# The mixing stage's normalised rows one place sooner in the loop that all engines share

## What is computed

```python
h = jnp.maximum(_layernorm(x, axis=-1), 0.0)
x = x + _L0_gnn_ref(h, adj, ...)      # attention, 16 heads
h = jnp.maximum(_layernorm(x, axis=-1), 0.0)
x = x + _L1_gnn_ref(h, adj, ...)      # two steps of spreading and of top-p attention
h = jnp.maximum(_layernorm(x, axis=-1), 0.0)
x = x + _L2_gnn_ref(h, adj, ...)      # attention, 8 heads, then four dense layers
h = jnp.maximum(_layernorm(x, axis=-1), 0.0)
x = x + _L3_gnn_ref(h, adj, ...)      # relations
```

```python
# end of L1: Z holds the sums of both steps
Y = X + Z
mu = Y.mean(axis=-1, keepdims=True)
var = Y.var(axis=-1, keepdims=True)
return (Y - mu) * jax.lax.rsqrt(var + LN_EPS) * gamma + beta
# next: x = x + that;  h = relu(_layernorm(x));  and of L2:
Wh = jnp.einsum('nf,hfd->hnd', x, W)
e_src = jnp.einsum('hnd,hd->hn', Wh, a1)
e_dst = jnp.einsum('hnd,hd->hn', Wh, a2)
```

## Time and profile before

| what | value |
|---|---|
| median of 3 runs | 3774.04 us |
| the three runs | 3775.52, 3774.04, 3762.97 us |
| the profiled execution | 3772.07 us, its span 3770.3 us |
| mean granted TensorE clock | 0.952 |
| busy share of the span | PE 90%, DVE 85%, ACT 75%, POOL 37% |
| the stage of the change | about 2328 to 2465 us of the span |

### The profile page before, as it was taken

The page is one execution under the profiler, slowest core; times in us unless marked ns, Lnnn a source line. Parts: engine busy times, 40 slices in busy tenths (PEclk is TensorE's granted clock), DMA queues, the critical chain, the costliest instruction groups (busy, mean ns, idle before and its releaser), DMA issues. The chain is left out here.

```text
span 3770.3 us, 56703 instructions
## 1 busy us (share of the span) xinstructions
PE 3378.9 (90%) x20628; PEld 2047.1 (54%) x20628; DVE 3201.0 (85%) x5502; ACT 2818.1 (75%) x3508; POOL 1389.7 (37%) x1048
## 2 busy tenths in 40 slices
PE   7799999986968976899999975989999898999999
PEld 3699999743434433444444432468888443444444
DVE  3699999679999999599999998389998414999996
ACT  5699999559999999389999982368776334666664
POOL 0387444104555556136565552145552110000000
PEclk9999999998989988999999987999999999999999
DMA  6721111120111113221101022410100211111110
GB/s 234 269 84 31 31 36 25 52 70 27 54 32 42 42 44 102 78 81 46 39 20 28 26 73 70 154 26 21 21 22 10 86 72 61 48 51 56 48 51 17
DMA packets 166328, 224.45 MB, mean 60 GB/s; under 512 B 90418, under 2 KB 102672, under 8 KB 162928
## 3 DMA queue, kind: packets, MB, share of 16 engines
q1 hardware_dynamic: 147152, 178.22, 15.1%
q0 software_dynamic: 18896, 42.46, 3.5%
HBM read 148.36 MB, written 72.00 MB: 58 GB/s over the span
## 5 line engine op out<-in xcount | busy, mean ns | idle before, releaser
L1819 DVE SCALAR_TENSOR_TENSOR adjT<-adjT,mid 128x2048 bf16<-128x2048 f32 x440 | 1034.8, 2352 | 13.9
L604 ACT ACTIVATE steepz<-s1b,thr_h 128x512 bf16<-128x512 f32 (+1 forms) x928 | 774.3, 915 | 32.5 <-DVE A L675 20.3
L1715 ACT ACTIVATE adjT<-adjT,nmid 128x2048 bf16<-128x2048 f32 x250 | 498.4, 1994 | 3.4 <-POOL nmid L1757 3.4
L1719 ACT ACTIVATE adjT<-adjT 128x2048 bf16<-128x2048 bf16 x250 | 477.9, 1912 | 6.0
L758 PE MATMUL acc<-V,B 128*128 128x198 bf16 x4096 | 442.5, 251 | 34.2 <-DVE B L677 14.1
L765 PE MATMUL acc<-V,adjT 128*128 128x99 bf16 (+1 forms) x5248 | 415.5, 217 | 0.0
L1773 POOL TENSOR_SCALAR reach<-above,lack 128x1 f32<-128x1 f32 x202 | 234.2, 1159 | 472.9 <-ACT lack L1722 472.7
L1775 POOL TENSOR_SCALAR nmid<-reach,steps,nmid 128x1 f32<-128x1 f32 x202 | 369.4, 1829 | 21.2
L765 PEld LDWEIGHTS acc<-V,adjT 128*128 128x128 bf16 x5248 | 340.5, 98 | 40.2 <-issue 0.7
L758 PEld LDWEIGHTS acc<-V,B 128*128 128x128 bf16 x4096 | 341.2, 98 | 37.6 <-issue 23.3
L1574 PE MATMUL psX<-parts,block 128*128 128x512 bf16 x1536 | 347.9, 382 | 10.5 <-POOL ident L209 4.1
(11 more groups left out here) (322 smaller groups left out, 6214.2 us busy)
## 6 DMA issues: line engine op xcount, KB each, us to landing
rows<-in_adj_dram SPq DMA_DIRECT2D x16, 1024.0 KB, 8.3
s1b<-sT_dram SPq DMA_DIRECT2D x32, 512.0 KB, 3.7
block<-adj_dram SPq DMA_DIRECT2D x32, 512.0 KB, 4.4
plain_table<-rows POOLq DMA_DIRECT2D x16, 512.0 KB, 8.1
adj_dram<-adjT POOLq DMA_DIRECT2D x4, 2048.0 KB, 21.6
veil_table<-fill POOLq DMA_DIRECT2D x64, 128.0 KB
y_dram<-yo SPq DMA_DIRECT2D x32, 256.0 KB, 2.0
adjT<-adj_dram SPq DMA_DIRECT2D x4, 2048.0 KB, 16.4
```

The lines of the kernel that those rows point to most:

```text
L604: act.activation(steepz[:, m % RELUS, :], s1b[:, q % 4, :], ACT.Relu, bias=thr_h[:, u, 1, j:j + 1], scale=STEEP).then_inc(relu_ready, 1)
L1715: act.activation(junk_s[:, u, :], expd[:, slot[i], :], ACT.Relu, bias=col(nmid, i), accum_out=col(above, i)).then_inc(sums_ready, 1)
L1719: act.activation(junk_s[:, u, :], junk_s[:, u, :], ACT.Sign, accum_out=col(over, i)).then_inc(sums_ready, 1)
L1819: link(dve.scalar_tensor_tensor(junk[:, :], e, col(mid, i), e, ALU.is_gt, ALU.mult, accum_out=found))
```

## The change

One number changes. `SOON` is 6 in place of 7 (LAG is 9), and with it `BEHIND` is 9 in place of 10 and the place of the last scores (`SOON + NT`) 22 in place of 23. The places of the late tiles' turns and sums, and all of VectorE's, GpSimd's and SyncE's order, stay.

```diff
             psS = psT[:, 0, :, :].rearrange("p k i -> p (k i)")[:, 0:NT * 2 * H].rearrange("p (t h) -> p t h", t=NT)
             m2 = psO[:, 1, 0:H]
-            SOON = LAG - 2
+            SOON = LAG - 3
             BEHIND = SOON + 3
             scored = {18 - 2: 0, 20 - 2: 1, 22 - 2: 2, SOON + NT: 3}
```

## The result

| | before | after |
|---|---|---|
| median, 9 executions each | 3772.60 us | 3787.28 us |
| lowest and highest | 3762.97, 3777.34 us | 3777.90, 3792.59 us |
| the profiled execution | 3772.07 us | 3792.59 us |
| the stage of the change | 137.81 us | 152.49 us |

The ratio is 1.0038, with a 95% interval of 1.0028 to 1.0047: slower, by 14.7 us. It grew by 14.68 us in the two profiled executions. That this is the difference of the medians to 0.01 us is chance: by the interval the medians differ by 10.6 to 17.7 us, and the length of a stage scatters too, as the experiments show.

What follows compares the result with a forecast made beforehand. TensorE's first start, work and idle time bound the stage. New stretches 6.35 + 6.78, less 4.44 gained, give +8.7 us; the clock's 4.4 makes +13.1, from 3774.04 to 3787.1, taken as 3787.0 us; range 3778 to 3792.

Steps and rivals of the forecast that it cites:

- The line of 0.3%: Whole kernel: a measurement can tell about 0.3%, 11.3 us, from no change; the forecast lies just beyond.
- The stage lasts as long as first start, work and idle time.: TensorE in the stage: the change alters no operation, so only first start (2352.50 us) and idle stretches can move time.
- The first start does not move.: Stage start: relu 0 still waits for VectorE's offsets, so the first turn keeps its time; put at zero.
- 4.44 us go.: Old TensorE idle stretches ahead of turns 3, 4 and 7 go or are counted anew: 1.74 + 0.54 + 2.16 us gained.
- 6.35 and 6.78 us come.: New TensorE idle stretches ahead of turn 4 (behind O9) and turn 8 (behind O12), waiting for group factors.
- The clock, 4.4 us.: Behind both new stretches TensorE's clock falls to half; matmuls there cost 2.2 us more each, +4.4 us.
- GpSimd meets VectorE in both chains.: GpSimd's addition again meets VectorE's `nmr` in both chains, keeping it at 1.20 us, not 0.16; 2.1 us in all.
- faster: Rival at relu 4: factors ready when O9 ends, old stretches go and none come; 3769.6 us, chance 0.03.
- The clock holds: Rival behind the new stretches: idle time comes as computed, clock stays full; +8.7 us, 3782.7 us, chance 0.11.
- More than two stretches: Rival in the stage: a shifted late sum opens a third idle stretch; +19.5 us, 3793.5 us, chance 0.06.
- The next stage absorbs it: Rival behind the stage: attention waits for the adjacency matrix, so a later end is free; 3774 us, chance 0.04.
- One sign that the prediction set: Outside the stage: the forecast is wrong if other stages differ by more than 2 us.

Runs made afterwards that it cites:

- The first experiment: Changed kernel, but VectorE takes the factors of tiles 4 to 7 ahead of its look at tile 9; stage 141.56 us, median 3776.86 us, ratio 0.9998.
- The kernel with both loops opened: Changed kernel, VectorE taking factors of tiles 4-7 before look 9, of 8-11 before look 12; GpSimd's additions for tiles 7, 11, 15 wait for factors; 3766.80 us.
- the filler: Changed kernel plus six unused 128x512 float32 products on TensorE ahead of turn 4 and of turn 8; stage 146.24 us, median 3782.77 us, ratio 1.0021.
- the third experiment: Changed kernel, but GpSimd's additions for tiles 7, 11 and 15 wait for VectorE's factors of the group before; stage 148.40 us, median 3784.29 us, ratio 1.0024.
- the repaired kernel: Changed kernel, SOON 6, factors of tiles 4-7 before look 9 and of 8-11 before look 12, GpSimd's three additions waiting; stage 132.55 us, ratio 0.9983.

## Why the prediction was right

The forecast was 3787.0 us and +13.1 us; measured were 3787.28 us and +14.7 us. That the level agrees within 0.3 us is luck: the difference was 1.6 us too small, and the kernel before came out at 3772.60 in place of 3774.04 us. The line of 0.3% that the prediction drew lies within the measured interval (1.0028 to 1.0047), so on which side of it the change fell is not settled. Step by step:

- *The stage lasts as long as first start, work and idle time.* It held for the dependences: in all kernels the stage grew and shrank by starts and waits. But "TensorE's work" is no constant, since the clock makes it longer, at the start too.
- *The first start does not move.* Right, the first turn comes 23.80 us into the stage in both. From it to the end of O8, though, the changed kernel took 9.09 us in its profiled execution. In the kernel before it was 2360.36 - 2352.50 = 7.86 us; with turn 2 (0.44 us), which now stands ahead of O8 and not behind it, 8.30. So +0.8 us came here that the prediction put at zero. The new order is not shown to be the reason: six kernels of this order took 8.26 to 9.09 us, and the two of the old order, with the 0.44 us, 8.30 and 8.82. The clock rose at another time in each profiled execution, and the prediction had no term for that.
- *4.44 us go.* Right: no waits ahead of turns 3 and 7. The recorded reason for turn 3 names the wrong instruction: relu 3 stood behind the root of tile 8 (2361.61 us), but what held it until 2365.42 were the roots of tiles 4 to 7, directly ahead of it on ScalarE before the change.
- *6.35 and 6.78 us come.* Right: 6.29 and 6.76. The first experiment shows the cause of the first by taking it away alone. The kernel with both loops opened shows it for both.
- *The clock, 4.4 us.* Its mechanism was right and its size too small: 2.60 + 2.86 = 5.46 us here, shown by the filler to be the clock. Behind stretches of 5.3 to 6.8 us the fall cost 2.60, 2.86, 1.85, 2.95, 1.85, 2.55 and 2.83 us in four kernels, 2.5 us on average where the prediction took 2.2, and a single one can't be told better than to some 0.6 us. The price did not follow the length of the stretch: 1.85 us stood behind 6.76 us of idle time and 2.95 us behind 5.26.
- *GpSimd meets VectorE in both chains.* Right, and shown by the third experiment to be worth 1.04 us each time. It meets VectorE a second time in the chain behind O12, at L141, which the prediction did not name; the 6.78 us, read from the trace, held it all the same.

The rows of the kernel before on which two of these readings rest, the end of O8 and the roots ahead of relu 3:

```profile
2359.34 1.02 PE L2014 MATMUL psO<-parts,ident 128*128 128x512 f32 x2
```

```profile
2365.31 0.21 ACT L146 ACTIVATE sd<-veps 128x4 f32<-128x4 f32 x1 [3.50 <-DVE veps L141]
```

The sum with measured terms is 6.29 + 6.76 - 4.44 + 5.46 + 0.8 = 14.9 us, against 14.68 in the stage.

Of the rivals, "faster" (3769.6 us) is excluded, since the whole interval lies above 1; its mechanism, factors ready when O9 ends, is what the repaired kernel has. "The clock holds" is what the filler made: +8.4 us in the stage. "More than two stretches" did not come: TensorE's other two waits in the stage are 1.53 and 1.16 us before and after. "The next stage absorbs it" did not come either: from the stage's end to the end of the span it took 1303.8 us before and 1307.3 us after.

One sign that the prediction set was too tight, and by its letter the forecast would be wrong: the stages outside this one should not differ by over 2 us. They differed by 2.3 us ahead of the stage and by 3.5 us behind it. The stage began at 2328.70 us before and at 2331.00 after, and in the other profiles anywhere from 2325.46 to 2331.92, with the same program ahead of it; behind it the other profiles took 1298.0 to 1306.9 us. So one pair of executions gives the size of this change only to some 10 us by its times; the length of the stage gives it more closely.

## What to carry to other kernels

When engines share a loop in which each handles a different tile, as in the kernels here, moving one step a place sooner is safe only if no released work depends, by way of other engines, on something the same engine has just issued. Walk the chain once around (matmul, statistics, factors, relu, turn), take its length from the trace, and compare it with the work that the new order leaves between its two ends: here 6.35 us against nothing and 11.09 against 4.31. If the chain is longer, shorten it by letting the engine that sums up a group do so before it looks at the next tile; the earlier place then pays, here with 1.7 us. Do so only for the groups whose loop closes: with the first group too the stage was 0.7 us longer, and with all groups it won nothing against the kernel before.

## What was not expected

- The price of a fall of TensorE's clock did not follow how long TensorE had waited, nor when in the wait the clock fell. In the changed kernel it had fallen late in the first stretch (a mean of 0.88 over 6.3 us is 1.5 us at 0.50) and earlier in the second (0.66 over 6.5 us is 4.4 us at 0.50), and the prices were 2.60 and 2.86 us. What sets the price stays open. Work that no result needs, put into the two stretches, was worth 5.5 us here.
- An earlier start can be taken back by the clock. Where the first turns came 3.4 and 3.8 us sooner but with gaps between them, the same work took 10.0 us up to the end of O8, 0.9 to 1.7 us longer than without the gaps, at 0.50 until about 2359 us in both.
- At the stage's start the same instructions took from 8.26 to 9.09 us to the end of O8 in six kernels that have the same order there, by when the clock rose; the stage's length can't be compared more closely than that from one profile.
